# X transposed of the next Newton-Schulz iteration as a product of X and B, row loads one by one, and a new list of steps

## The chip, the cores and the metric

The kernel runs on one core of a Trainium2 chip (trn2), as one program with one launch. The metric is device time in microseconds (us). The time of the kernel before is the median of three runs. TensorE (PE in the profile; PEld is its weight loads), VectorE (DVE), ScalarE (ACT), GpSimd (POOL) and SyncE (SP, which issues all DMAs) each work through their own instruction stream in order, and wait for each other by semaphores.

## The reference: what is computed

x has 4 batches, 512 tokens and 256 columns, all float32. A layer norm is followed by two branches: causal window attention (2 heads of 128, blocks of 128 tokens), and a test-time-training layer with 16 small networks (4 batches x 4 heads, weights W0, W1, W2 of 64x64 each). Their sum goes through Wo, a layer norm and the residual; then a feed-forward part (256 to 1024 to 256, exact GELU), a layer norm and a residual. The tokens go in 4 chunks of 128. After each of the first three chunks the 48 weights are changed by a gradient that five Newton-Schulz iterations make nearly orthogonal:

```
for a, b, c in NS_COEFFS:          # five of them
    A = X @ X.T
    B = b * A + c * (A @ A)
    X = a * X + B @ X
```

The next chunk needs the new weights, so this chain (five iterations, three chunks) is serial.

## The kernel before

All data stay in SBUF. One list, ORDER (lines 136 to 183), names 687 steps such as `NA.0.1.2` (kind NA, chunk 0, iteration 1, group 2). Every engine walks through that same list and does its own part of each step; so the list sets the order on each engine, and each engine waits by semaphores for what the others make. `bank_plan` gives each step its PSUM bank, or a pair of banks, from the list; the PE part of a step waits until the bank's last reader is done (`take`, `take_pair`).

The three groups (0: W1, 1: W2, 2: W0) hold 16 matrices of 64x64 each. An iteration of a group is four steps. TX (line 670; ACT part 946) transposes X by four 128x128 matmuls against the identity, and ACT copies the result into XT. NA (681) multiplies XT by itself, DVE (1242) makes A. NB (691) squares A, DVE (1249) makes B. NX (701; ACT 950) multiplies B and X, and ACT writes the new X; in the last iteration DVE writes U (the weights plus the update) instead. NA, NB and NX are 16 logical products of 64x64, spread over the four quadrants of the array (QUADS); the profile has two records for each of them, so 32 matmul records and 32 weight loads for a step, and 4 and 4 for TX.

After the last iteration RN and RM normalize the rows of U with a square root on POOL (a power, line 1406) and small DVE operations, then WX transposes the new weights. Before the first, MU, MR, SS and SN make the Frobenius norm (POOL power) and X. Beside this chain, the list places the projections of the next chunk (XT, QK, VV, TR), attention (S, PT, PV, CT), WO, NT, and the feed-forward (F1, line 769, and F2, line 783) of this chunk, as filling for PE. The steps FW, DH, GB, OUT, EL, ELB and DW are the small networks' forward and backward parts. F2N, the last step of a row block, subtracts and scales on DVE (1370), adds the residual on POOL (1511), and SP stores the block.

SP issues the loads: x of chunk 1 (`rows_in(1)`) after the weights of the small networks, then p1T, p2T, wo and x again for the residual (`rows_again`). For later chunks `rows_in` and `rows_again` are one DMA of 512 KB each; those of chunk 3 and chunk 2 follow the four stores of chunk 0. At the start, PE does eight matmuls on a tile of ones (line 803) before its first real work.

Of the kernel before, what the change touches and what calls it, by code (L numbers as in the profile page):

```python
# [26 lines left out]
ALU = mybir.AluOpType  # L27
# [3 lines left out]
P = 128  # L31
# [3 lines left out]
HD = 64  # L35
# [39 lines left out]
class Signal:  # L75
# [53 lines left out]
def steps(text):  # L129
# [22 lines left out]
    TR.1.7 TR.1.8 NX.0.4.0 NX.0.4.1 NX.0.4.2 RN.0.0 RN.0.1 RN.0.2 RM.0.0 RM.0.1 TR.1.9 KL.1.0 KL.1.1 RM.0.2 SP.1 S.1.1
    F2.0.1 F2.0.2 DH.1 WX.1.0 WX.1.1 WX.1.2 KL.1.2 KL.1.3 F2.0.3 FE.1.0 FE.1.1 EL.1.0 EL.1.1 FW.1.0 FW.1.1 ELB.1.0
    ELB.1.1 GB.1.0 GB.1.1 OE.1 QK.2.0 QK.2.1 OUT.1.0 OUT.1.1 MU.1.0 MU.1.1 MU.1.2 MR.1.0 MR.1.1 DW.1.0 DW.1.1 PT.1.0
    PT.1.1 MR.1.2 QK.2.2 S.1.2 QK.2.3 SS.1.0 SS.1.1 OY.1 SS.1.2 S.1.3 VV.2.0 PV.1.0 SN.1.0 SN.1.1 VV.2.1 PT.1.2 PV.1.1
    PT.1.3 SN.1.2 TX.1.0.0 PV.1.2 PV.1.3 CT.1.0 CT.1.1 TX.1.0.1 TX.1.0.2 NA.1.0.0 NA.1.0.1 NA.1.0.2 WO.1.0 WO.1.1
    CT.1.2 WON.1.0 CT.1.3 WON.1.1 SI.2.0 NB.1.0.0 NB.1.0.1 NB.1.0.2 L2.1.0 NQ.2.0 L2.1.1 L2N.1.0 WO.1.2 WO.1.3 TR.2.0
    NX.1.0.0 NX.1.0.1 NX.1.0.2 TX.1.1.0 NT.1.0 VV.2.2 TX.1.1.1 TX.1.1.2 WON.1.2 NA.1.1.0 NA.1.1.1 NA.1.1.2 SI.2.1
    NB.1.1.0 NB.1.1.1 WON.1.3 L2.1.2 TR.2.1 TR.2.2 TR.2.3 VV.2.3 NB.1.1.2 L2.1.3 NX.1.1.0 NX.1.1.1 L2N.1.1 NX.1.1.2
    L2N.1.2 TX.1.2.0 TX.1.2.1 TX.1.2.2 L2N.1.3 NT.1.1 NT.1.2 NT.1.3 NQ.2.1 NA.1.2.0 NA.1.2.1 NA.1.2.2 SI.2.2 SI.2.3  # L160
    F1.1.0 F1.1.1 NQ.2.2 NQ.2.3 NB.1.2.0 NB.1.2.1 NB.1.2.2 MS.2 F2N.0.0 F2N.0.1 F1.1.2 F1.1.3 F2N.0.2 NX.1.2.0 F2N.0.3
# [5 lines left out]
    GB.2.1 PT.2.0 OY.2 EL.2.0 EL.2.1 QK.3.0 ELB.2.0 ELB.2.1 MU.2.0 MU.2.1 MU.2.2 MR.2.0 QK.3.1 MR.2.1 MR.2.2 PT.2.1
    DW.2.0 DW.2.1 QK.3.2 SS.2.0 S.2.2 S.2.3 SS.2.1 SS.2.2 PV.2.0 PV.2.1 QK.3.3 CT.2.0 CT.2.1 SN.2.0 PT.2.2 TX.2.0.0
    SN.2.1 SN.2.2 WO.2.0 TX.2.0.1 TX.2.0.2 NA.2.0.0 NA.2.0.1 NA.2.0.2 NB.2.0.0 NB.2.0.1 NB.2.0.2 VV.3.0 PT.2.3
    NX.2.0.0 NX.2.0.1 NX.2.0.2 F2N.1.0 F2N.1.1 F2N.1.2 TX.2.1.0 TX.2.1.1 WON.2.0 PV.2.2 TX.2.1.2 F2N.1.3 SI.3.0  # L170
    NA.2.1.0 NA.2.1.1 NA.2.1.2 CT.2.2 PV.2.3 WO.2.1 NB.2.1.0 NB.2.1.1 NB.2.1.2 CT.2.3 WON.2.1 WO.2.2 WO.2.3 NX.2.1.0
# [5 lines left out]
    NB.2.4.2 TR.3.4 F1.2.2 NX.2.4.0 NX.2.4.1 NX.2.4.2 RN.2.0 RN.2.1 RN.2.2 MS.3 TR.3.5 F1.2.3 F1.2.4 F1.2.5 F1.2.6
    WX.3.0 WX.3.1 WX.3.2 F1.2.7 RM.2.0 RM.2.1 RM.2.2 FE.3.0 FE.3.1 FW.3.0 FW.3.1 PT.3.0 OE.3 S.3.2 S.3.3 OUT.3.0
    OUT.3.1 PT.3.1 F2.2.0 OY.3 PV.3.0 F2.2.1 PT.3.2 PT.3.3 PV.3.1 PV.3.2 CT.3.0 PV.3.3 CT.3.1 CT.3.2 WO.3.0 WO.3.1
    WO.3.2 CT.3.3 WON.3.0 WON.3.1 L2.3.0 L2.3.1 L2N.3.0 L2N.3.1 F2.2.2 F2.2.3 NT.3.0 NT.3.1 WO.3.3 WON.3.2 WON.3.3  # L180
# [1377 lines left out]
```

## Time and profile before

| | |
|---|---|
| median of 3 runs | 387.1 us (386.88 to 387.57) |
| profiled execution, its own time | 388.49 us |
| profiled execution, span from first to last instruction | 386.7 us, granted clock 0.999 |
| busy: PE, PEld, DVE, ACT, POOL | 369.2, 294.9, 271.5, 219.2, 191.7 us |
| chain that ended last: PE | 83% of the span |

The profiled execution has 1.8 us around its span. Busy time is the time covered by at least one instruction of the engine. Ends of matmuls are modelled, so a short wait can hide under the modelled end of the matmul before it.

### The profile page before, as it was taken

The numbers are of one execution on the slowest core, as the hardware profiler recorded it, in microseconds if no ns is written. First come the engines' busy times: TensorE is split into PE (matmuls) and PEld (weight loads), VectorE is DVE, ScalarE is ACT, GpSimd is POOL, SyncE is SP. The second block draws the span as 40 slices with busy tenths as digits, with TensorE's granted clock in tenths as the row PEclk, the third lists the DMA queues.
The fourth block names the chain that finished last, engine by engine and source line by source line (L and its number), as shares of the span: only waits on it lengthen the run. The fifth ranks groups of instructions, "written<-read, shape, count | busy, mean of one in ns | idle before, by whom it ended". The sixth has DMA issues, their size and how long they took to land.

```text
span 386.7 us, 15982 instructions
## 1 busy us (share of the span) xinstructions
PE 369.2 (95%) x6758; PEld 294.9 (76%) x6758; DVE 271.5 (70%) x729; ACT 219.2 (57%) x436; POOL 191.7 (50%) x267
## 2 busy tenths in 40 slices
PE   6969999999999999999997999999999999999994
PEld 4558678866689877988577788779888756998883
DVE  4587998735589689877665976997785583676223
ACT  1798386576453467476756336674458966524410
POOL 5486952414437755473463666553362331456323
PEclk9999999999999999999999999999999999999999
DMA  5770000000000000000050000000300000000101
GB/s 153 232 234 25 3 1 3 3 4 3 3 4 2 2 3 0 4 4 4 3 159 11 4 2 2 2 3 17 99 5 3 3 4 2 1 3 0 57 14 41
DMA packets 12342, 10.85 MB, mean 28 GB/s; under 512 B 4208, under 2 KB 11760, under 8 KB 12272
## 3 DMA queue, kind: packets, MB, share of 16 engines
q1 hardware_dynamic: 12272, 9.83, 8.3%
q8 instruction: 54, 0.88, 1.0%
q14 instruction: 16, 0.13, 0.1%
HBM read 7.73 MB, written 2.10 MB: 25 GB/s over the span
## 4 chain that ended last, share of the span: by engine, by line
PE 83%; DVE 8%; issue 3%; POOL 3%; ACT 2%; POOLq 0%; DVEq 0%; ACTq 0%
PE pair L788 14%; PE pair L777 14%; PE pair L708 6%; PE pair L686 6%; PE pair L696 5%; PE pair L677 5%; PE pair L558 5%; PE pair L743 3%; PE pair L586 3%; PE pair L758 3%; PE pair L567 3%; PE pair L727 3%; PE pair L734 2%; PE pair L657 2%; PE pair L624 1%
## 5 line engine op out<-in xcount | busy, mean ns | idle before, releaser
L777 PE MATMUL pair<-xn2T,p1T 128*128 128x512 f32 (+1 forms) x160 | 59.2, 513 | 0.0
L788 PE MATMUL pair<-p2T,h 128*128 128x256 f32 x256 | 57.0, 379 | 0.0
L788 PEld LDWEIGHTS pair<-p2T,h 128*128 128x128 f32 x256 | 48.1, 190 | 6.3
L1411 POOL TENSOR_SCALAR var<-mv 128x1 f32<-128x1 f32 (+1 forms) x55 | 14.1, 256 | 67.4 <-DVE mv L1367 30.5
L1029 ACT ACTIVATE h<-pair,b 128x512 f32<-128x512 f32 (+1 forms) x40 | 24.1, 602 | 35.5 <-PE pair L777 35.5
L777 PEld LDWEIGHTS pair<-xn2T,p1T 128*128 128x128 f32 x160 | 28.8, 190 | 17.6 <-issue 15.5
L1406 POOL TENSOR_TENSOR nq<-ssq,half 128x8 f32<-128x8 f32 (+1 forms) x16 | 23.8, 1498 | 37.2 <-DVE ssq L1128 37.1
L1052 DVE SCALAR_TENSOR_TENSOR A<-pair,eye 128x512 f32<-128x512 f32 x45 | 28.5, 680 | 11.1 <-PE pair L686 11.1
L1406 POOL TENSOR_TENSOR rstd<-var,neg_half 128x1 f32<-128x1 f32 (+1 forms) x55 | 32.9, 598 | 4.6
L820 ACT ACT_TABLE_LOAD x26 | 33.4, 1283 | 2.1 <-PEq L1548 1.7
L1052 DVE SCALAR_TENSOR_TENSOR B<-pair,eye 128x512 f32<-128x512 f32 x45 | 28.4, 681 | 6.5 <-PE pair L696 6.3
L558 PE MATMUL pair<-wqkv,xnT 128*128 128x512 f32 x64 | 29.7, 600 | 0.6 <-ACT xnT L813 0.6
L708 PEld LDWEIGHTS pair<-X,B 64*64 64x64 f32 x1440 | 23.6, 134 | 7.9 <-issue 4.5
L696 PEld LDWEIGHTS pair<-A 64*64 64x64 f32 x1440 | 23.4, 134 | 6.4 <-issue 5.1
L708 PE MATMUL pair<-X,B 64*64 64x64 f32 x1440 | 25.8, 221 | 2.0 <-issue 2.0
L954 ACT ACTIVATE X<-pair 128x512 f32<-128x512 f32 x36 | 19.5, 597 | 14.3 <-PE pair L708 14.1
L686 PEld LDWEIGHTS pair<-XT 64*64 64x64 f32 x1440 | 22.8, 135 | 4.6 <-issue 4.6
L696 PE MATMUL pair<-A 64*64 64x64 f32 x1440 | 25.7, 221 | 0.2 <-DVE A L1052 0.2
L813 ACT ACTIVATE XT<-pair 128x512 f32<-128x512 f32 x45 | 24.4, 597 | 2.6 <-PE pair L677 2.5
L686 PE MATMUL pair<-XT 64*64 64x64 f32 x1440 | 25.1, 220 | 0.6 <-issue 0.6
L677 PE MATMUL pair<-ident,X 128*128 128x128 f32 x180 | 24.0, 276 | 0.0
L1406 POOL TENSOR_TENSOR fro<-ss,half 128x8 f32<-128x8 f32 x9 | 15.9, 1781 | 13.4 <-DVE ss L1223 13.4
(163 smaller groups left out, 785.7 us busy)
## 6 DMA issues: line engine op xcount, KB each, us to landing
x<-in_L_attn_x_dram SPq DMA_DIRECT2D x4, 512.0 KB, 4.3
out_dram<-rows_a SPq DMA_DIRECT2D x16, 128.0 KB, 1.7
x_in<-in_L_attn_x_dram SPq DMA_DIRECT2D x3, 512.0 KB, 4.7
p1T<-in_L_ffn_proj_dram SPq DMA_DIRECT2D x1, 1024.0 KB, 6.0
p2T<-in_L_ffn_proj_dram SPq DMA_DIRECT2D x1, 1024.0 KB, 8.3
wqkv<-in_L_attn_Wqkv_dram SPq DMA_DIRECT2D x1, 768.0 KB, 4.5
x_in<-in_L_attn_x_dram SPq DMA_DIRECT2D x4, 128.0 KB, 4.3
wo<-in_L_attn_Wo_dram SPq DMA_DIRECT2D x1, 256.0 KB, 8.6
```

The lines of the kernel that those rows point to most:

```text
L558: mm_ = pe.matmul(ps, xnT[:, k, b * P:(b + 1) * P], wqkv[:, k, 0:512], start=(k == 0), stop=(k == KC - 1))
L677: mm_ = pe.transpose(ps[:, b * P:(b + 1) * P], X[:, g, 2 * b:2 * b + 2, :], ident[:, :])
L686: mm_ = pe.matmul(BANK[bank[0] + row][64 * col:64 * col + 64, n * HD:(n + 1) * HD], xt, xt, start=True, stop=True)
L696: mm_ = pe.matmul(BANK[bank[0] + row][64 * col:64 * col + 64, n * HD:(n + 1) * HD], a, a, start=True, stop=True)
L708: mm_ = pe.matmul(BANK[bank[0] + row][64 * col:64 * col + 64, n * HD:(n + 1) * HD], B[64 * row:64 * row + 64, g, 4 * (row ^ (slot & 1)) + ...
L777: mm_ = pe.matmul(ps[:, at], p1T[:, k, n * P:(n + 1) * P], xn2T[:, k, at], start=(k == 0), stop=(k == KC - 1))
L788: mm_ = pe.matmul(ps[:, 0:DIM], h[:, n, b * P:(b + 1) * P], p2T[:, n, :], start=(n == 0), stop=(n == HC - 1))
L813: return act.activation(dst, src, ACT.Copy)
L820: act.preload_act_table_set(name)
L1029: act.activation(h[:, n, at], BANK[bank[0]][:, at], ACT.Gelu, bias=b1[:, n:n + 1]).then_inc(S["h"].sem, 1)
L1052: return dve.scalar_tensor_tensor(out=out_, in0=in0, scalar=scalar, in1=in1, op0=op0, op1=op1)
L1406: return pool.tensor_tensor(out_, in0, in1, op)
```

## The change

TX is kept for the first iteration only. For the others a new step XX makes XT of the next iteration directly from X and B, with the operands of NX exchanged (B is symmetric, so the product of X and B is the transpose of B X); it writes a pair of banks, and ACT scales it as it scales X. XX(it) and NX(it) both wait for B(it) and, from it = 1 on, for X of the iteration before. NA of the next iteration needs XX alone. SP issues each 512 KB of rows as four DMAs of 128 KB, each one after the landing of the one before (without that wait for x of chunk 1). Some small operations are dropped or moved: the scaled maximum of the scores comes straight out of the masking reduction, the sums of an epsilon in NR and SN go from DVE to POOL, RM has one operation fewer, in the last chunk F2N is done on DVE alone with its subtraction ahead of the wait for the scale, the constants come in another order, and PE does seven matmuls on ones instead of eight. ORDER is a new list of 689 steps.

```diff
-    XT.0.0 LN1.0.0 LNX.0.0 LN1.0.1 LN1.0.2 QK.0.0 LN1.0.3 LNX.0.1 XT.0.1 SI.0.0 LNX.0.2 LNX.0.3 VV.0.0 QK.0.1 XT.0.2
...
-    NX.0.1.0 NX.0.1.1 L2.0.2 L2.0.3 NX.0.1.2 NT.0.0 NT.0.1 NT.0.2 TX.0.2.0 TX.0.2.1 L2N.0.1 L2N.0.2 L2N.0.3 TX.0.2.2
-    NT.0.3 NA.0.2.0 NA.0.2.1 NA.0.2.2 F1.0.0 F1.0.1 NB.0.2.0 NB.0.2.1 NB.0.2.2 F1.0.2 NQ.1.0 NQ.1.1 F1.0.3 LN1.2
...
+    CO.0 XT.0.0 LN1.0.0 LNX.0.0 QK.0.0 LN1.0.1 LN1.0.2 LN1.0.3 XT.0.1 LNX.0.1 LNX.0.2 LNX.0.3 SI.0.0 VV.0.0 VV.0.1
+    NQ.0.0 XT.0.2 XT.0.3 QK.0.1 SI.0.1 WI.0 LN1.1 NR.0.0 VV.0.2 VV.0.3 NQ.0.1 QK.0.2 LNX.1 MS.0 SI.0.2 QK.0.3 SM.0
+    NQ.0.2 SI.0.3 NQ.0.3 XT.1 SP.0 TR.0.0 TR.0.1 TR.0.2 NR.0.1 VV.1.0 NR.0.2 NR.0.3 TR.0.3 KL.0.0 WX.0.0 WX.0.1 WX.0.2
...
+    F1.0.3 LN1.2 NX.0.1.1 NB.0.2.1 NX.0.1.2 NB.0.2.2 NX.0.2.0 NB.0.3.0 F1.0.4 XX.0.2.1 NR.1.3 XX.0.2.2 XX.0.3.0 TR.1.4
+    LNX.2 F1.0.5 KL.1.0 NA.0.3.1 NA.0.3.2 KL.1.1 KL.1.2 NA.0.4.0 XT.2 F1.0.6 NX.0.2.1 NX.0.2.2 NB.0.3.1 NB.0.3.2
...
+    F1.3.7.0 F1.3.0.1 F1.3.1.1 F2N.2.1 F1.3.2.1 F1.3.3.1 F1.3.4.1 F1.3.5.1 F1.3.6.1 F1.3.7.1 F2N.2.2 F2N.2.3 F2.3.0
+    F2.3.1 F2.3.2 F2N.3.0 F2N.3.1 F2.3.3 F2N.3.2 F2N.3.3

 def rows_again(c):
-    sp.dma_start(x1[:, c % 2, :, :], rows(c)).then_inc(S["x_again"].sem, 16)
+    for b in range(BATCH):
+        if b:
+            sp.wait_ge(*S["x_again"](c, 16 * b))
+        sp.dma_start(x1[:, c % 2, b, :], x[b, bass.ts(c, CHUNK), :]).then_inc(S["x_again"].sem, 16)

 # PE, NX: one more wait
+    if it > 0:
+        pe.wait_ge(*S["X"](c, 3 * (it - 1) + g + 1))

+def XX(bank, c, it, g):
+    take_pair(bank[0], "XT", c, 3 * (it + 1) + g + 1)
+    if it > 0:
+        pe.wait_ge(*S["X"](c, 3 * (it - 1) + g + 1))
+    pe.wait_ge(*S["B"](c, 3 * it + g + 1))
+    for n in range(4):
+        for row, col in QUADS:
+            half, k = n & 1, 2 * (n >> 1) + col
+            slot, at = ns_slot(it, g, half, k), (2 * (n >> 1) + half) * HD
+            mm_ = pe.matmul(BANK[bank[0] + row][64 * col:64 * col + 64, at:at + HD],
+                            X[64 * row:64 * row + 64, g, slot, :],
+                            B[64 * row:64 * row + 64, g, 4 * (row ^ (slot & 1)) + (slot >> 1), :], start=True, stop=True)
+    mm_.then_inc(S["xt_ps"].sem, 1)

 # ACT
+def XX(bank, c, it, g):
+    act.wait_ge(*S["xt_ps"](c, 3 * (it + 1) + g + 1))
+    act.activation(halves(XT[:, g, :, :]), both(bank[0]), ACT.Copy, scale=NS_REST[it]).then_inc(S["XT"].sem, 1)

-for n in range(8):      # PE, matmuls on ones
+for n in range(7):

 # DVE, RM: three small operations become two, with row_inv = 1 / row_norm made once (step WR)
-    dve.tensor_scalar(u_e[:, g, :], u_n[:, g, :], 1e-5, None, ALU.add).then_inc(S["u_eps"].sem, 1)
+    stt(u_e[:, g, :]..., u_n[:, g, :]..., 1e-5, row_inv[:, g, :]..., ALU.add, ALU.mult).then_inc(S["u_eps"].sem, 1)
...
-    dve.tensor_scalar(nmax[:, b, :], smax[:, b, :], -SCALE, None, ALU.mult).then_inc(S["neg_max"].sem, 1)

 # DVE, F2N of the last chunk
+    dve.tensor_scalar(f2_n[:, b, :], f2[:, b, :], mv4[:, b, 0:1], None, ALU.subtract).then_inc(S["f2_n"].sem, 1)
+    wait_apart(dve, S["f2_n"](c, b + 1))
+    dve.wait_ge(*S["f2_rstd"](c, b + 1))
+    stt(outb[:, b, :], f2_n[:, b, :], rstd4[:, b:b + 1], x1[:, c % 2, b, :], ALU.mult, ALU.add).then_inc(S["outb"].sem, 1)
```

## Rows read from the trace of the kernel before

**Rows 1.** The page: busy us (share) and count by engine.

```profile
PE 369.2 (95%) x6758; PEld 294.9 (76%) x6758; DVE 271.5 (70%) x729; ACT 219.2 (57%) x436; POOL 191.7 (50%) x267
```

**Rows 2.** Waits of PE: line, releaser: us in total, times, longest.

```profile
PE pair L542 <- DVE rows_b L1081: 2.3, 1, 2.3
PE pair L708 <- issue: 2.0, 1, 2.0
PE pair L586 <- POOL silu L1406: 1.3, 1, 1.3
...
PE pair L686 <- issue: 0.6, 1, 0.6
```

**Rows 3.** Waits of the weight loads (PEld), same columns.

```profile
PEld pair L708 <- DVE B L1052: 2.8, 5, 0.8
```

**Rows 4.** The chain in order of time: start us, us, what.

```profile
59.63 1.67 PE pair L686 x96
...
66.31 1.09 PE pair L708 x64
...
79.67 1.31 PE pair L677 x12
...
94.16 1.72 PE pair L777 x4
...
98.04 1.56 PE pair L686 x96
99.60 3.63 PE pair L777 x8
...
104.78 1.86 PE pair L708 x96
```

**Rows 5.** Timeline, 0 to 34 us: start us, us, engine, instruction [idle before].

```profile
3.06 3.75 PE L803 MATMUL pair<-ones 128*128 128x128 f32 x16 [3.06 <-DVE ones L1389]
...
5.35 0.41 DVE L1074 TENSOR_SCALAR rows_b<-x_in,mv,rstd 128x256 f32<-128x256 f32 x1 [1.12 <-POOL rstd L1406]
...
12.25 0.59 SPq L457 DMA_DIRECT2D x_in<-in_L_attn_x_dram  x1
...
19.70 1.36 DVE L1064 BATCH_NORM_STATS2 st<-x_in 128x6 f32<-128x256 f32 x4
```

**Rows 6.** The page, DMA issues: count, KB each, us to landing.

```profile
x_in<-in_L_attn_x_dram SPq DMA_DIRECT2D x3, 512.0 KB, 4.7
```

**Rows 7.** Timeline, 374 us to the end, same columns.

```profile
382.15 0.18 DVE L1367 BATCH_NORM_AGGREGATE mv<-st 128x2 f32<-128x6 f32 x1
...
383.40 0.41 DVE L1372 TENSOR_SCALAR rows_a<-rows_a,mv,rstd 128x256 f32<-128x256 f32 x1 [1.07 <-POOL rstd L1406]
383.89 0.72 POOL L1406 TENSOR_TENSOR rows_a<-rows_a,x 128x256 f32<-128x256 f32 x1 [0.53 <-DVE rows_a L1372]
```

**Rows 8.** Groups of instructions: names xcount | busy us, mean ns | idle.

```profile
L1134 DVE TENSOR_SCALAR nqe<-nq 128x8 f32<-128x8 f32 x12 | 5.6, 470 | 0.7 <-POOL nq L1406 0.7
...
L1289 DVE TENSOR_SCALAR nmax<-smax 128x2 f32<-128x2 f32 x16 | 3.2, 198 | 0.6
```

**Rows 9.** Timeline, 196 to 209 us: row loads, and the wait of PE.

```profile
198.01 0.46 SPq L452 DMA_DIRECT2D x<-in_L_attn_x_dram  x1
...
198.52 0.54 SPq L457 DMA_DIRECT2D x_in<-in_L_attn_x_dram  x1
...
205.72 1.63 PE L708 MATMUL pair<-X,B 64*64 64x64 f32 x96 [2.03 <-issue]
```

**Rows 10.** The page, DMA queues over the span: packets, MB, share.

```profile
q8 instruction: 54, 0.88, 1.0%
```

**Rows 11.** The DMA view of 197.2 to 203.2 us, same columns.

```profile
q1 hardware_dynamic: 1324, 1.29, 70.5%
```

**Rows 12.** The DMA view of 203.2 to 204.3 us, same columns.

```profile
q8 instruction: 1, 0.02, 5.6%
```

**Rows 13.** Busy by engine, 264 to 304 us: length, PE, PEld, DVE, ACT, POOL, clock.

```profile
264.00:304.00 40.00, 40.00 (x1244) 34.61 (x1240) 28.90 (x74) 24.08 (x47) 16.90 (x29) 1.00 0.10 30
```

More of the change, by code:

```diff
@@ L152 @@
[L152 to L161, printed above, removed]
@@ L167 @@
[L167 to L171, printed above, removed]
@@ L177 @@
[L177 to L180, printed above, removed]
-    L2.3.2 L2.3.3 L2N.3.2 L2N.3.3 F1.3.0.0 F2N.2.0 F2N.2.1 F2N.2.2 F2N.2.3 F1.3.1.0 F1.3.2.0 F1.3.3.0 F1.3.4.0
@@ new lines @@
+    LNX.2 F1.0.5 KL.1.0 NA.0.3.1 NA.0.3.2 KL.1.1 KL.1.2 NA.0.4.0 XT.2 F1.0.6 NX.0.2.1 NX.0.2.2 NB.0.3.1 NB.0.3.2
+    F1.0.7 NX.0.3.0 NB.0.4.0 XX.0.3.1 XX.0.3.2 TR.1.5 TR.1.6 TR.1.7 TR.1.8 MP.1 WR.0 SP.1 KL.1.3 TR.1.9 NA.0.4.1
+    NA.0.4.2 F2.0.0 NX.0.3.1 NX.0.3.2 NX.0.4.0 NB.0.4.1 NB.0.4.2 F2.0.1 NX.0.4.1 RN.0.0 RN.0.1 NX.0.4.2 RN.0.2 RM.0.0
+    RM.0.1 RM.0.2 F2.0.2 F2.0.3 F2N.0.0 WX.1.0 WX.1.1 WX.1.2 DH.1 FW.1.0 FW.1.1 FE.1.0 FE.1.1 EL.1.0 EL.1.1 GB.1.0
+    GB.1.1 ELB.1.0 ELB.1.1 OUT.1.0 OUT.1.1 PT.1.0 OE.1 QK.2.0 QK.2.1 QK.2.2 DW.1.0 DW.1.1 MU.1.0 MU.1.1 MU.1.2 MR.1.0
@@ L188 @@
           "F1": 1, "F2": 1, "SS": 1, "TX": 1, "WX": 1}
-PAIRED = ("NA", "NB", "NX", "GB", "FW", "DH", "OUT")
+PAIRED = ("NA", "NB", "NX", "XX", "GB", "FW", "DH", "OUT")
 def last_reader(step, n):
@@ L1048, in _ @@
         def _(dve):
+            dve.memset(ones[:, :], 1.0).then_inc(warm, 1)
             for name in RAISED_AHEAD["vector"]:
@@ L1052, in stt, with CO @@
                 return dve.scalar_tensor_tensor(out=out_, in0=in0, scalar=scalar, in1=in1, op0=op0, op1=op1)
+            def CO(c):
+                dve.memset(small_bias[:, 0:12], BASE_LR_INV)
+                dve.memset(ones_avg[:, :], 0.5 / CHUNK)
+                for r in range(2):
+                    for k in range(2):
+                        last = dve.memset(ones_blk[64 * r:64 * r + 64, 64 * k:64 * k + 64], float(r == k))
+                last.then_inc(prepared, 1)
             def LN1(c, b=None):
@@ L1387, in run @@
                         parts[kind](c, *arg)
-            dve.memset(ones[:, :], 1.0).then_inc(warm, 1)
-            dve.memset(neg_half[:, :], -0.5)
-            dve.memset(half[:, :], 0.5)
-            dve.memset(small_bias[:, 0:12], BASE_LR_INV)
-            dve.memset(ones_avg[:, :], 0.5 / CHUNK)
-            for r in range(2):
-                for k in range(2):
-                    last = dve.memset(ones_blk[64 * r:64 * r + 64, 64 * k:64 * k + 64], float(r == k))
-            last.then_inc(prepared, 1)
             run(ORDER)
```

139 lines of the change are left out of this document (78 added, 61 removed).

## The prediction

> **What bounds the kernel now.** I read the page's busy row first, then the waits of PE, then the chain in order of time, and the timeline where the chain leaves PE. The row shows PE covered for 369.2 of 386.7 us and DVE for 271.5 [rows 1]. So the time is PE's own work plus the places where PE waits. The waits of PE [rows 2] are few: at the start for the normalized rows of chunk 1 (2.3 us) and for POOL's scaled q and k (1.3), and in the middle 2.0 and 0.6 us of "issue", waits that no semaphore explains. The weight loads [rows 3] show what the modelled ends of matmuls hide: 2.8 us in 5 places behind DVE's B. The start (first real matmul at 6.6 us) and the tail behind the last matmul (5.6 us) are serial and have their own chains.
>
> **PE's own work.** The chain gives step prices [rows 4]: three quadrant steps in a row take 1.56 us, two take 1.09, so one more costs 0.47. Three transpose steps TX take 1.31, so 0.44 each. XX replaces TX 36 times (iterations 0 to 3, 3 groups, 3 chunks): 36 x 0.03 = +1.1 us. XX has the matmuls of NX, 16 products on quadrants, and I price it as NX; exchanging the two operands leaves all shapes at 64x64. From below: TX's own price, +0. From above: a step of a triple with the slow spacing, 1.86 / 3 = 0.62 [rows 4], +6.5. I take 0.47, the undisturbed row.
>
> A run of quadrant steps between steps on the whole array costs something at its borders. F1 after a quadrant triple: two steps in 3.63 us, where one alone takes 1.72, so 0.19 for the borders, and the triple takes 1.56 where 3 x 0.47 is 1.41, so 0.15 more: 0.34 us a run [rows 4]. Counting both lists, the quadrant steps (NA, NB, NX, XX, FW, DH, OUT) stand in 51 runs in the old one and in 57 in the new one: +2.0 us. That XX does away with the whole-array TX inside an iteration does not pay here, because the new list spreads the groups more finely. Together PE's work grows by 3.1 us. The Trainium skill says the same of the borders (TensorEngine Tiling (Array Packing), Key Properties: a change of tiling mode drains the engine), and speaks against this change, as it would against any list with more runs; it names no price, and the 0.34 is the trace's.
>
> PE also has one more semaphore wait ahead of NX and up to two ahead of XX (63 in all for the X of the iteration before). That X was written by ACT one iteration earlier, several us of PE work ago, so nothing is waited for. The instruction itself is taken in ahead of the matmuls: nothing, at most 0.05 us each, the difference of two such borders, so 3 us at most.
>
> **Start.** The first transpose starts at 6.61, though its rows are written at 5.35 + 0.41 = 5.76: it stands behind the eight matmuls on ones, 3.75 us long [rows 5]. One less is 3.75 / 8 = 0.43 to 0.47 us earlier, just what the rows allow: -0.4 us, if the clock is granted as before. After it PE runs without a wait to about 18.7 (its work there is the same as now, where it first waits at 18.3). Now XT.1 comes next instead of TR.0.0. Its rows: x of chunk 1 is issued from 12.25 on and lands 4.7 us later [rows 5, 6], near 17; statistics on DVE 1.36 + 0.4 [rows 5], two small POOL operations 1.3, normalization on DVE as long as the statistics, the copies of VV lying between: about 21.9. So PE waits 3.2 us in one place and 1 us for ACT's copy behind it, and TR.0.0 to TR.0.2 are queued behind the waiting XT.1 though they are ready. Against that, the waits before XT.1 (2.3) and TR.0.4 (1.3) go [rows 2], with a shorter one before TR.0.0, and three VV steps fill the time for POOL's chain, which gets 4 additions of 0.26 us longer. Followed further by the same durations (EL and ELB now ahead of OE on DVE, so DW is 1.5 us earlier against the work; OE ahead of MU, so the momentum is later), NA.0.0.0 comes out at 59.5, as now at 59.63 [rows 4]. So: 0, between -1.5 and +1.5.
>
> **Tail.** Before: aggregate 382.15 + 0.18, POOL's scale, DVE 383.40 + 0.41, POOL 383.89 + 0.72 = 384.61, then the store [rows 7]. Now F2N.3.2 follows F2.3.3 on DVE, two operations of 0.41, then F2N.3.3's subtraction and product, again 2 x 0.41: from 382.4 with three gaps, 384.2. -0.4 us, between -0.8 (F2N.3.2 fits in earlier) and 0.
>
> **Small operations.** DVE loses 16 maxima of 0.2 us, 16 additions of 0.47 [rows 8], and some 18 of 0.16; about 12 us of its busy time. PE does not wait for most of them; the long ones (0.47 is a mean over 0.15 and about 1 us) hold A and B back in a dense place. I count this in the next part. POOL gets 25 additions of 0.26 and is half idle: 0. RM's saved operation lies in a chain for which the new list leaves 7.8 us or more of other PE work against about 5.8: 0.
>
> **Waits in the iterations.** This is where the change can win. (a) Row loads: two 512 KB DMAs are issued at 198.01 and 198.52, and PE, with no semaphore open, stands still for 2.03 us before 205.72 [rows 9]. From 197.2 to 203.2 only the queue of the data has packets [rows 11]; one packet of the queue "instruction" follows at 203.2 to 204.3 [rows 12]. The kernel has 54 of them, 0.88 MB [rows 10], for 2 x 6758 PE instructions [rows 1], so one per 250. I read it as PE's code waiting behind the rows. With at most 128 KB under way this cannot last: -2.0 us; from above 0, if the code is late for another reason. (b) Consumers close behind producers: by the step prices, 51 places in the old list have under 1.3 us of PE work between the end of NA, NB, NX or TX and the step that needs it (a DVE or ACT operation of 0.6 to 0.68 and two hand-overs take about 1.0), 17 in the new one. What that costs shows in the triple at 104.78, 1.86 instead of 1.56, and in rows 3: 2.8 us of B waits, and some for A. Part of these lies under matmuls still draining; between 0.3 (what the matmul rows show) and 4 I take 2.4 now and 0.8 after: -1.6. Fewer close places come from the shorter chain, since NA needs XX alone and NX can come late.
>
> Sum: 3.1 - 0.4 + 0 - 0.4 - 2.0 - 1.6 = -1.3 us. The profiled span of 386.7 becomes 385.4, its own time of 388.5 becomes 387.2; the median of the runs, 387.1, becomes 385.8. About 0.2% (0.8 us) is what a measurement tells from no change.
>
> **Rivals.** First, PE's code becomes the bound, and the kernel is slower. XX has 64 matmuls and weight loads where TX has 8: +56 x 36 = 2016 instructions, 8 blocks more, all in the iterations. In the 40 us from 264 to 304 PE has 1244 matmul and 1240 load records [rows 13], a block in 4.0 us, and no such wait. The wait of 0.6 us inside an NA step [rows 2], with no row load near, says that a denser stretch (there about 3.1 us for a block) is already too fast. With 56 more for each XX the mean there falls to about 3.3 us for a block. If a block needs 3.7 (0.6 more than 3.1), the mean shortfall is 0.4, but only where the list is dense: of some 45 blocks in the iterations I count 12, 4.8 us, which come on top of -1.3, less 0.6 for close places that the waits then cover: 390.0. It decides from a block time under about 3.5 us on. For it: the 0.6 us, and runs of six to nine quadrant steps in the new list. Against it: that wait is one in 54 blocks. The Trainium skill (Runtime: NRT & Kernel Launch, Instruction fetch mechanics) calls the cost of passing from one 16 KiB block to the next mostly hidden; by that rule this rival is worth nothing and the 2.0 us are due to something else, but the trace's two waits disagree.
>
> Second, the gains cancel: the 2.0 us are not the row loads' doing, or the wait returns elsewhere. Now the four loads of rows take about 4 x 2.2 us one after the other, twice, next to the densest steps of chunk 1. Then 3.1 - 0.8 - 1.6 + 0.6 = +1.3 at most, and with half of it 387.2. For it: a single wait is the evidence.
>
> Third, the start goes better than followed: three VV steps earlier leave PE ahead of DVE, and 1.5 to 2 us of the start's waits go: 384.0. Against it: DVE is nearly full from 40 to 60 us, and its order sets the first X.
>
> That XX does not shorten the chain at all can be left out: NA's wait is on XT alone, and one PE step and one ACT copy are gone from each iteration.
>
> **Chances.** The forecast 0.44, with its own range 384.5 to 387.0; code as the bound 0.28 (387.8 to 392); cancelled 0.20 (386.4 to 388.2); a better start 0.08. Faster by over 0.2%, below 386.3: 0.35 + 0.08 + 0.03 = 0.46; within 0.2%: 0.09 + 0.13 + 0.02 = 0.24; slower: 0.30. Range for 8 in 10: 383.2 to 390.5; it leaves out the worse part of the first rival and the sum of all lower bounds.
>
> **What would show it.** PE's busy count must rise by about 2000 matmul and load records and the instruction queue by 8 packets. Right: XX triples at 1.56 us; no wait of PE over 1 us while rows are loaded; NA.0.0.0 near 59.5; the end 5.2 us behind the last matmul. The first rival shows as "issue" waits of PE in front of or inside NA, NB, NX and XX, of 3 us or more in total, each with an instruction packet shortly before its end. A dearer XX (0.5 or more), or a start over 1.5 us later, would also make the prediction wrong.

## The result, and the profile after

The changed kernel takes 396.65 us (median of three runs, 395.9 to 399.36) against 387.1 us before (386.88 to 387.57): ratio 1.0235, interval 1.0191 to 1.0279. It is slower by 9.5 us and lies outside the range of the prediction (383.2 to 390.5). Its profiled execution has a span of 394.5 us, 7.8 us more than before, and 2.15 us around it. Here and below, ratios and intervals are taken over the fast runs alone (in e1, e3 and e4 one run of four was slow), so a ratio is not the quotient of the two medians.

The page after, in its busy row and the row of the instruction queue, to be read beside [rows 1] and [rows 10]:

```profile
PE 375.5 (95%) x7764; PEld 298.1 (76%) x7764; DVE 261.1 (66%) x682; ACT 216.7 (55%) x433; POOL 194.4 (49%) x290
...
q8 instruction: 62, 1.02, 1.1%
```

PE has 1006 matmuls and as many weight loads more, and eight instruction packets more, as forecast. DVE lost 10 us. The waits of PE, as in [rows 2]:

```profile
PE pair L544 <- DVE rows_b L1111: 3.3, 1, 3.3
...
PE pair L695 <- issue: 1.4, 1, 1.4
PE pair L695 <- ACT XT L974: 1.0, 1, 1.0
PE pair L709 <- issue: 0.8, 1, 0.8
PE pair L676 <- DVE X L1263: 0.6, 2, 0.3
PE pair L560 <- ACT xnT L829: 0.6, 1, 0.6
PE pair L781 <- DVE A L1073: 0.5, 1, 0.5
```

L695 is NB and L709 NX in the changed kernel. The 2.0 us before NX are gone; in their place stand 1.4 and 0.8 us of "issue" and 1.0 us behind ACT's copy of XT, all in chunk 2. The iterations of chunk 2, from NA.2.0.0 to NX.2.4.2, in the windows of the kernel before (columns as in [rows 13]):

```profile
263.00:312.90 49.90, 49.90 (x1557) 41.80 (x1560) 35.62 (x93) 33.15 (x62) 18.31 (x32) 1.00 0.08 25
```

The same stretch of the kernel after:

```profile
263.30:319.50 56.20, 52.22 (x1887) 43.05 (x1887) 35.44 (x89) 31.06 (x61) 17.30 (x33) 1.00 0.03 9
```

PE was covered throughout before and has 4 us of holes after, with nothing busier than it. The largest hole, in the timeline of the changed kernel:

```profile
273.24 1.04 PE L695 MATMUL pair<-A 64*64 64x64 f32 x43
...
275.68 0.98 PE L695 MATMUL pair<-A 64*64 64x64 f32 x51 [1.40 <-issue]
```

It lies inside the step NB.2.1.0, which waits for semaphores only ahead of its first matmul, so no semaphore can be the cause: the step's first part is done, and its next record starts 1.6 us later.

**A place in the instruction stream.** If all of PE's records are numbered from 0 in order of start (matmuls, weight loads, and the semaphore instructions, which the page doesn't count: 13945 before, 15964 after), the waits of over 0.7 us in the iterations that no semaphore explains have one thing in common:

| kernel | wait ends at record | modulo 256 | us between starts |
|---|---|---|---|
| before | 1985 | 193 | 0.79 |
| before | 7873 (the 2.0 us of [rows 9]) | 193 | 2.10 |
| after | 11969 | 193 | 1.62 |
| after | 14017 | 193 | 1.00 |

The instruction queue has 62 packets of 16 KB for the 15964 records after (257 for each) and 54 for the 13945 before (258 for each). I read it so: every 256 records PE crosses into a block of code whose packet must be there. I call the place a crossing. The numbering starts at the first record that the trace shows, and instructions ahead of it would shift it; so the period of 256 says something, and the 193 by itself does not. The packet of the wait at 275.68 had run from 272.92 to 274.22 (DMA view of 272.9 to 274.3 us of the kernel after):

```profile
q8 instruction: 1, 0.02, 5.8%
```

From 274.2 to 275.6 no queue had a packet at all, and PE went on 1.46 us after its packet had ended. The two waits of chunk 2 have the same sequence: the packet starts 1.1 to 1.4 us after the crossing ahead of it, takes 0.9 to 1.3 us, and 1.2 to 1.5 us after its end PE goes on. In the iterations of both kernels the crossings are 3.45 us apart at the least, and nearly all 3.6 or more: **a block costs about 3.7 us at least**, on the mean of a dense stretch. That is an estimate and no hard floor: single blocks are shorter in the experiments (down to 1.9 us in e3 and e4, 2.9 in e1, 3.2 in e12), and the 86 blocks of all traces that end in a wait of over 0.3 us take 4.0 in the median, since a packet can also start late. Eight quadrant steps of 64 instructions take 3.7 us and hold two blocks.

The Trainium skill (Runtime: NRT & Kernel Launch, Instruction fetch mechanics) calls the cost of crossing a block mostly hidden. The traces agree where 256 instructions last longer than that (all crossings of the kernel before but two, whose packets started 2.3 and 3.8 us after the crossing ahead); in runs of quadrant steps they do not.

**Where the 7.8 us are.** I took the time between the first matmuls of neighbouring steps, less the step prices of the prediction and 0.34 us for each run of quadrant steps. From NA.0.0.0 on:

| us | before | after |
|---|---|---|
| places over 0.12 us with a crossing in them | 3.7 | 4.4 |
| places over 0.12 us without one | 2.1 | 7.3 |

Besides these there are +1.1 us of work for XX, six runs more (+2.0 by the price of the prediction, which nothing measures by itself), -0.2 at NA.0.0.0 (59.63 to 59.45) and -0.4 in the tail. That adds up to 8.4 us, 0.6 more than measured. The crossings hide a change of kind: the 1.9 us beside the row loads went, and 2.8 us came in chunk 2. The places without a crossing are 1.24 us in one (NB.2.3.0, whose banks wait for ACT's copy of XT), and some twenty of 0.12 to 0.6 us, half of them in chunk 2.

### The profile page after: what moved, and what is told of

Same layout as the page of the kernel before. It is cut to its first block, busy times and chain, and to the rows that moved or that the text cites. A ratio compares the mean times of both kernels' runs of the same rounds, so it can differ in the third digit from the quotient of the medians.

```text
span 394.5 us, 17995 instructions
## 1 busy us (share of the span) xinstructions
PE 375.5 (95%) x7764; PEld 298.1 (76%) x7764; DVE 261.1 (66%) x682; ACT 216.7 (55%) x433; POOL 194.4 (49%) x290
## 4 chain that ended last, share of the span: by engine, by line
PE 74%; DVE 9%; issue 5%; POOL 4%; ACT 3%; SPq 3%; DMA 1%; POOLq 0%; DVEq 0%; ACTq 0%
PE pair L793 13%; PE pair L804 12%; PE pair L695 5%; PE pair L709 5%; PE pair L685 5%; PE pair L724 4%; PE pair L588 4%; PE pair L560 4%; PE pair L774 3%; PE pair L759 3%; PE pair L743 3%; PE pair L569 2%; PE pair L750 2%; POOL rstd L1430 2%; PE pair L659 1%
## 5 line engine op out<-in xcount | busy, mean ns | idle before, releaser
L1435 POOL TENSOR_SCALAR var<-mv 128x1 f32<-128x1 f32 (+1 forms) x55 | 12.2, 222 | 79.2 <-DVE mv L1393 43.8
L1073 DVE SCALAR_TENSOR_TENSOR B<-pair,eye 128x512 f32<-128x512 f32 x45 | 29.9, 685 | 18.9 <-PE pair L695 18.6
L709 PEld LDWEIGHTS pair<-X,B 64*64 64x64 f32 x1440 | 24.8, 135 | 8.6 <-issue 7.0
L695 PE MATMUL pair<-A 64*64 64x64 f32 x1440 | 28.2, 220 | 2.9 <-issue 1.4
L709 PE MATMUL pair<-X,B 64*64 64x64 f32 x1440 | 28.8, 221 | 0.8 <-issue 0.8
L970 ACT ACTIVATE X<-pair 128x512 f32<-128x512 f32 x36 | 20.9, 596 | 15.3 <-PE pair L709 15.3
L974 ACT ACTIVATE XT<-pair 128x512 f32<-128x512 f32 x36 | 20.3, 596 | 14.8 <-PE pair L724 14.7
L695 PEld LDWEIGHTS pair<-A 64*64 64x64 f32 x1440 | 24.7, 135 | 4.7 <-issue 2.8
L685 PE MATMUL pair<-XT 64*64 64x64 f32 x1440 | 27.2, 221 | 0.5 <-DVE wo_n L1346 0.2
L1430 POOL TENSOR_TENSOR kl<-silu,lr 128x256 f32<-128x256 f32 x24 | 14.3, 618 | 25.6 <-issue 25.6
L1389 DVE TENSOR_TENSOR rows_a<-pair,b 128x256 f32<-128x256 f32 x16 | 6.6, 415 | 27.1 <-PE pair L804 27.1
```

The lines of the kernel that those rows point to most:

```text
L685: mm_ = pe.matmul(BANK[bank[0] + row][64 * col:64 * col + 64, n * HD:(n + 1) * HD], xt, xt, start=True, stop=True)
L695: mm_ = pe.matmul(BANK[bank[0] + row][64 * col:64 * col + 64, n * HD:(n + 1) * HD], a, a, start=True, stop=True)
L709: mm_ = pe.matmul(BANK[bank[0] + row][64 * col:64 * col + 64, n * HD:(n + 1) * HD], B[64 * row:64 * row + 64, g, 4 * (row ^ (slot & 1)) + ...
L970: act.activation(halves(X[:, g, :, :]), both(bank[0]), ACT.Copy, scale=NS_REST[it]).then_inc(S["X"].sem, 1)
L974: act.activation(halves(XT[:, g, :, :]), both(bank[0]), ACT.Copy, scale=NS_REST[it]).then_inc(S["XT"].sem, 1)
L1073: return dve.scalar_tensor_tensor(out=out_, in0=in0, scalar=scalar, in1=in1, op0=op0, op1=op1)
```

## The experiments

Each ran beside the kernel before on the same chip; the ratio is to it. "From NA.0.0.0 to the end" is the time from that step's first matmul to the end of PE's work in the profiled execution: 321.5 us before, 329.9 after. It leaves the start out.

**e1, the crossings shifted.** Against the kernel before:

```diff
-for n in range(8):   pe.matmul(BANK[7][...128...], ones, ones)
+for n in range(6):   pe.matmul(BANK[7][...128...], ones, ones)
+for n in range(26):  pe.matmul(BANK[7][0:64, 0:64], ones[0:64, 0:64], ones[0:64, 0:64])
```

> The kernel before, with its eight matmuls on ones at the start replaced by six of them and 26 small ones of 64x64. That puts 96 more PE instructions ahead of the first real one, in about the same 3.6 us; list, waits and work are unchanged. Theory S (supply of PE's instructions): in both traces the waits of PE over 0.7 us that no semaphore explains end at the same place of its instruction stream, counted in all PE records: 193 modulo 256 (records 1985 and 7873 before; 11969 and 14017 after; one at 13484 is at 172). So every 256 instructions PE crosses into a block that must have been fetched, and between two crossings at least about 3.7 us must pass. Shifting the crossings by 96 puts several of them into dense runs of quadrant steps. Worked out from the step prices: +11 us, 398, with single waits of 1.3 to 1.9 us inside steps near NX.0.3.2, NX.1.3.2, NB.2.0.1 and NB.2.3.2, each again at 193 modulo 256. Rival L (what costs is the list: borders between quadrant and whole-array steps, consumers close behind producers): list and steps are unchanged, so 387.1 within 0.5 us.

Measured: 408.4 us, ratio 1.045 (1.036 to 1.054). The profiled execution is the fastest of the four (402.8 us; the others took 408.3 to 409.6, and no trace shows where their last 5.6 us are). In it NA.0.0.0 to the end takes 333.4 us, 11.9 more than before (forecast 11); the first matmul came 2.5 us later besides. Twelve waits over 0.3 us end at 193 modulo 256, 13.5 us together. The waits of PE:

```profile
PE pair L696 <- issue: 3.7, 3, 1.7
PE pair L708 <- issue: 3.1, 4, 1.8
PE pair L686 <- issue: 2.4, 3, 1.0
```

All four steps named have a wait in them (0.6, 2.0, 1.1 and 1.3 us between starts). Rival L is out: with an unchanged list the time grew by more than the change itself had cost.

**e2, the control: a whole block more.** 4 matmuls on ones and 68 small ones.

> The kernel before with 256 more small PE instructions at the start (four matmuls on ones and 68 of 64x64 instead of eight on ones), one whole block. The control for the shift of 96: more instructions, but every crossing at the same step as before. Theory S: 387.1 to 387.8 (the small matmuls may end 0.3 us later than the eight). If added instructions cost by themselves, it is slower than the shift of 96.

Measured: 404.3 us, ratio 1.039 (1.033 to 1.045), but not for the crossings: from NA.0.0.0 to the end it takes 322.3 us, 0.8 more than before, and the only wait over 0.3 us at a crossing is the one of the row loads (1.83 us). The time was lost at the start, in the timeline:

```profile
5.03 14.77 PE L805 MATMUL pair<-ones 64*64 64x64 f32 x136
19.73 0.28 PEld L535 LDWEIGHTS pair<-ident,rows_b 128*128 128x128 f32 x2
```

My padding was 13 us dearer than planned, and NA.0.0.0 comes another 2.7 us later against it. As to its question the control holds: 256 instructions more don't cost in the body, 96 do.

**e3, the changed kernel shifted by 64.** 5 matmuls on ones and 18 small ones instead of 7.

> The changed kernel with 64 more PE instructions at the start (five matmuls on ones and 18 of 64x64 instead of seven on ones), the rest unchanged. Theory S: the crossings come 64 instructions earlier in the list, and now the dense runs of all three chunks hold one; worked out from the step prices +20 us or a little less, 412 to 418. Rival L: 396.6 within 0.5 us.

Measured: 413.4 us, ratio 1.062 (1.056 to 1.067), as forecast. From NA.0.0.0 on 344.9 us, 15.0 more than the changed kernel; 16 waits at 193 modulo 256, 19.0 us. Seven are in NB:

```profile
PE pair L695 <- issue: 7.9, 7, 1.5
PE pair L724 <- issue: 3.7, 4, 1.4
```

So the list as it stands suits one position of its crossings. Four instructions fewer, as the change has with seven matmuls on ones in place of eight, should not matter: by the same working a shift of up to some 50 in that direction is nearly free, and 16 the other way costs 6 us. Neither was run.

**e4, XX alone.** The kernel before, TX.c.it+1.g taken out and XX.c.it.g put ahead of NX.c.it.g:

```diff
-... NX.0.1.0 NX.0.1.1 L2.0.2 ... TX.0.2.0 TX.0.2.1 ...
+... XX.0.1.0 NX.0.1.0 XX.0.1.1 NX.0.1.1 L2.0.2 ...
```

> The kernel before with one thing of the change: TX of the iterations 1 to 4 is gone, and XX stands directly ahead of NX of the same group. List otherwise, row loads, small operations as before. 51 runs of quadrant steps as before, PE's work by the step prices +1.1 us. Theory S: eight more blocks, all in the dense runs, 20 or more crossings under 3.7 us: +18 to +27 us, 405 to 415. Rival L (the new list is what costs, XX itself only 36 times 0.03): 387 to 388.5. Rival C (the shorter chain helps where the list is as before): 385 to 387.

Measured: 413.5 us, ratio 1.062 (1.055 to 1.069). From NA.0.0.0 on 346.1 us, 24.6 more than before, and 24 waits at crossings sum to 25.0 us. Two of them, in the timeline (L692 is NB, L704 NX, L719 XX here):

```profile
211.95 0.62 PE L692 MATMUL pair<-A 64*64 64x64 f32 x25
214.29 1.29 PE L692 MATMUL pair<-A 64*64 64x64 f32 x71 [1.73 <-issue]
...
216.24 0.51 PE L704 MATMUL pair<-X,B 64*64 64x64 f32 x18
218.65 0.59 PE L704 MATMUL pair<-X,B 64*64 64x64 f32 x12 [1.90 <-issue]
```

Between two waits lie 256 records and about two microseconds of work. XX by itself is what is dear, by its number of instructions and not by its matmuls. With the new list (and the rest of the change) 24.6 becomes 8.4; but e3, the same list shifted by 64, stands at 23.4. So the runs do not tell how much the new list gains by putting filling between the dense steps and how much by the position of its crossings.

**e5, the row loads one by one, alone.** The `rows_in` and `rows_again` of the change's diff in the kernel before.

> The kernel before with only the row loads of the change: four of 128 KB one after another in place of each 512 KB. Theory S (PE needs a fetched block every 256 instructions): the crossing at 203.62 waited 2.10 us because its packet started only at 203.25, 3.8 us after the crossing before it, behind the two loads; with 128 KB under way at most it starts within 1 to 2 us, as the others do. So the wait goes and nothing takes its place: -2.0 us, ratio 0.995. If the loads are not the cause, or it returns at a later crossing: ratio 1.000 within 0.001.

Measured: 398.1 us, ratio 1.023 (1.018 to 1.027): slower by 9 us (by 7.2 in the trace from NA.0.0.0 on). Theory S was right on the crossing (no wait at 193 is left) and blind to what follows. The timeline of SyncE and VectorE:

```profile
200.41 7.18 SPq L455 DMA_DIRECT2D x<-in_L_attn_x_dram  x4
207.63 7.75 SPq L463 DMA_DIRECT2D x_in<-in_L_attn_x_dram  x4
...
217.08 1.41 DVE L1070 BATCH_NORM_STATS2 st<-x_in 128x6 f32<-128x256 f32 x4 [9.71 <-DMA x_in<-in_L_attn_x_dram]
...
219.66 1.13 PE L692 MATMUL pair<-XT 64*64 64x64 f32 x32 [8.10 <-issue]
```

Eight loads, in two sets of four in which each waits for the landing of the one before it, take 15 us. The rows of chunk 3 are there at 217 and not near 204; DVE waits 9.7 us for them, with A and lr queued behind, and NA waits 8.1 us (named "issue", at record 50 modulo 256, so no crossing).

**e6 and e7, the small parts.** e6 is the changed kernel with the old list, TX and 512 KB loads; e7 the same with the loads one by one.

> The changed kernel with the old list and without XX (TX in all iterations, no wait for X ahead of NX) and with the old 512 KB loads: what is left of the change is the small operations, the last chunk's F2N on DVE, the order of the constants and seven matmuls on ones instead of eight. Five PE instructions more than before in all (by the program), so the crossings lie as before. Expected -0.4 at the start, -0.4 in the tail, some 0 to 0.7 us of B and A waits from 12 us less on DVE: -0.8 to -1.5 us, ratio 0.996 to 0.998.

> All of the change but XX and the new list: small operations, tail, start and the row loads one by one, on the old list. If the parts add up: -2.0 and -0.8 to -1.5, so -2.8 to -3.5 us, ratio 0.991 to 0.993, and faster than both kernels. If the row loads' wait comes back elsewhere: as the kernel with the small operations alone.

Measured: e6 389.2 us, ratio 1.000 (0.997 to 1.003); e7 397.8 us, ratio 1.022 (1.017 to 1.027). Both expectations were wrong. The start (6.18 instead of 6.61) and the tail showed their 0.4 us in e6's trace, but its median didn't; e7 has e5's wait, 9.0 us between starts. One thing that eats the gain in e6's trace is the clock: 0.9 us behind the end of its wait of 1.9 us at the row loads, PE's granted clock falls to half (1.2 GHz of 2.4), where the kernel before has 1.00 behind its own wait of 2.1 us. The windows of e6:

```profile
205.40:208.80 3.40, 3.40 (x67) 3.28 (x58) 1.14 (x7) 2.40 (x5) 1.26 (x2) 0.50 0.02 5
```

The iterations of chunk 1 take 58.9 us there and 57.4 before. A stretch at 0.50 stands behind the waits at this place in e1, e2 and e4 too, and a longer one around the 8 and 9 us waits of e5 and e7. So a wait of PE can cost more than its own length.

**e8, the changed kernel with 512 KB loads.**

> The changed kernel with the row loads undone (512 KB each again). In the changed kernel the loads run from 170.4 to 185.7 us, beside crossings 4 us apart that have 0.3 to 0.4 us to spare. Theory S: the two large loads hold an instruction packet back by 3 us, so +1.5 to +3 us, 398 to 399.7, with one wait of 1.5 to 3 us at 193 modulo 256 between 170 and 185 us. If the size of the loads does not matter here: 396.6 within 0.5.

Measured: 396.9 us, ratio 1.020 (1.016 to 1.024), no different from the changed kernel. Its trace shows the wait forecast at crossing 27, but 0.88 us of it and not 1.5 to 3 (0.32 in the changed kernel). The new list has the stores, and so the loads, at 170 us and not at 198, so neither size of load comes late. That the loads one by one didn't do in the change what they do in e5 is the list's merit.

**e9 and e10, the load earlier.** Against the kernel before (e10: against e6):

```diff
 for c in range(CHUNKS - 2):
-    rows_in(c + 2)
+    if c == 0:
+        rows_in(2)
+        rows_in(3)
     stores(c)
```

> The kernel before with one line of SyncE moved: the 512 KB load of x for chunk 3 is issued ahead of the stores of chunk 0 (as soon as the rows of chunk 2 are normalized, near 110 us) and not behind them at 198.5. Only the second load for the residual stays at 198. Theory S with what the row loads one by one taught (the loads must be early, not small): the instruction packet at 203.25 starts about 2 us earlier, the 2.1 us wait at 203.6 goes, and VectorE has its rows long before it reads them: -1.8 to -2.1 us, ratio 0.995. If a load of 512 KB alone already holds the packet back: -0.5 or less, ratio 0.999 to 1.000.

> The same move with the small operations, the tail and the seven matmuls on ones of the change, on the old list with TX and loads of 512 KB. The small operations alone gave a ratio of 1.000 (0.997 to 1.003), so this should be as the move alone: -1.8 to -2.5 us, ratio 0.994 to 0.996, and the fastest of all kernels so far.

Measured: e9 386.9 us, ratio 0.997 (0.994 to 1.000), with 319.5 us from NA.0.0.0 on, 2.0 less than before: the forecast is met in the trace and in the medians (388.9 before on that chip), but the ratio says 1.2 us and its interval just reaches 1. e10 387.25 us, ratio 0.994 (0.992 to 0.997): **faster than both kernels**, by 2.2 us against before by the ratio and 1.6 by the medians; whether it beats e9 is not decided. Its twelve runs all have a granted clock of 0.997 or 0.998, where those of the kernel before beside it lie between 0.988 and 1.0; so a part of the gain may be the clock's. No wait of PE at a crossing over 0.3 us is left in its body; in e9 one is:

```profile
PE pair L688 <- issue: 0.6, 1, 0.6
```

**e11, chunk 2 back to the old list.** The changed kernel up to NA.2.0.0, then the old list with TX, and its crossings put where the step prices like them best.

> The changed kernel up to the first NA of chunk 2, and from there the old list with TX (672 PE instructions fewer), the last chunk's tail as in the change. Five matmuls on ones and 56 small ones on the four quadrants in turn at the start, so that the crossings fall where the step prices give the least stalls: 2.8 us in all, where the changed kernel has 6.8 by the same working. Theory S: 0.7 us less work and 4.0 us less stall than the changed kernel: near 392, ratio 1.010 to the kernel before. If chunk 2 is not where the change loses (rival: start and borders): 396.6 as the changed kernel.

Measured: 392.5 us, ratio 1.0075 (1.004 to 1.011): the time is as forecast. From NA.2.0.0 to NX.2.4.2 50.3 us, against 56.2 in the changed kernel and 50.0 before. So chunk 2 is where the change loses. But the reason given, 4 us fewer stalls at crossings, is not what its trace shows: the waits over 0.3 us there sum to 4.3 us in all, against 2.9 in the changed kernel and 4.4 in e13, the same program again. In chunk 2 they are 1.7 us, against 2.6 and 4.8; in chunks 0 and 1, where the shift moved them, they are more. The old list takes away XX's instructions and the new list's semaphore waits together, so e11 tells where, and not which of the two.

**e12, XT.1 behind TR.0.2.**

> The changed kernel with XT.1 moved behind TR.0.2, so that the ready transposes TR.0.0 to TR.0.2 run while the rows of chunk 1 are made. In the changed kernel PE waits 3.3 us for them, and then shows a granted clock of 0.72 from 22 to 28 us and transposes of twice the duration. If the start's loss reaches the end: -1 to -2 us, 394.6 to 395.6, no stretch under full clock in the start. If VectorE sets the first iteration anyway (NA.0.0.0 at 59.5 in both kernels): 396.6 within 0.5, and NA.0.0.0 within 0.5 us of 59.5.

Measured: 401.7 us, ratio 1.032 (1.029 to 1.036), 5 us slower than the changed kernel: outside both expectations. ACT now works on TR's tables and copies when XT.1 is ready, and PE waits longer for its copy:

```profile
PE pair L568 <- ACT xnT L828: 4.5, 1, 4.5
```

From NA.0.0.0 to the end nothing changed (330.0 us); NA.0.0.0 came at 63.3, against 59.4 in the changed kernel and 58.9 in e13. So it was not VectorE alone that set it, and the change's order of the start is the better one.

**e13 to e15, supply or semaphores in chunk 2.** e13 is the changed kernel again; e14 moves one filling step, e15 brings in another.

```diff
-... NX.2.2.0 NB.2.2.2 NB.2.3.0 F1.2.0 F2N.1.1 ...
+... NX.2.2.0 F1.2.0 NB.2.2.2 NB.2.3.0 F2N.1.1 ...           e14
+... NX.2.2.0 F1.2.0 NB.2.2.2 NB.2.3.0 F1.2.1 F2N.1.1 ...    e15
```

> The changed kernel itself, unchanged, as the base on the same chip for the two that follow: 396 to 398 us.

> The changed kernel with one filling step moved: F1.2.0 stands ahead of NB.2.2.2 instead of behind NB.2.3.0, two steps earlier. Open question: between NA.2.0.0 and NX.2.4.2 the changed kernel has 3854 PE instructions, 15.1 blocks, at 3.7 us a block 55.7 us, and takes 56.2. But waits at crossings (2.6 us) are only part of what it lost there; 1.24 us is a wait of NB.2.3.0 for ACT's copy of XT, which holds its banks, and about 1 us are smaller semaphore waits. Theory S (the supply sets the time there, other waits only lie within it): the 1.24 us wait goes, since 1.9 us of F1 now stand ahead of it, and a crossing a little later waits 1.2 to 1.9 us in its place; the stretch stays at 56.0 to 56.3 and the time at that of the changed kernel within 0.3 us. Rival B (the new list's semaphore waits are the cost by themselves): the stretch takes 55.0 and the kernel is 1.2 us faster.

> As the kernel before this one, and one F1 step more among the iterations of chunk 2: F1.2.0 ahead of NB.2.2.2, F1.2.1, F1.2.2 and F1.2.3 where F1.2.0, F1.2.1 and F1.2.2 stood; F1.2.3 is taken from behind NX.2.4.2, where five such steps cover the row norms. It brings 8 PE instructions and 1.9 us of work into the dense stretch. Theory S: the stretch grows by 0.3 to 0.8 us only, since the work fills what were waits for the supply, and the part behind it is 1.9 us shorter: -1.0 to -1.6 us against the changed kernel, unless WX.3 now waits for the norms. Rival B: the stretch grows by 1.9 less 1.2 us for the wait that goes, and the kernel is 1.2 us faster as well; the two kernels together tell them apart by the one before.

Measured: 397.5, 396.7 and 397.2 us; ratios 1.020 (1.017 to 1.024), 1.019 (1.014 to 1.023), 1.019 (1.015 to 1.023). The stretch from NA.2.0.0 to NX.2.4.2 took 58.6, 56.4 and 58.8 us. The wait for ACT's copy went in both:

```profile
PE pair L723 <- ACT h L1048: 1.1, 1, 1.1
PE pair L694 <- issue: 0.9, 1, 0.9
PE pair L708 <- issue: 0.9, 1, 0.9
```

These are the rows of e14, where another semaphore wait of the same size took its place, 3 us later. In e15 1.9 us more work and 1.24 us less of that wait lengthened the stretch by 0.2 against e13, while its waits at crossings stayed (4.8 and 4.9 us); the part behind it won 0.3 and not 1.9, since a crossing waited there (1.2 us of PE, 1.9 between starts). No gain of 1.2 us shows, which speaks against rival B, but the intervals (0.4% each way) and the base's own spread (56.2 and 58.6 us for one program) don't settle 1 us. Of the 2.4 us of that spread 2.2 lie in waits at crossings; without these waits the stretch takes 53.5 to 53.9 us in the changed kernel, e13, e14 and e15 alike.

## Why the prediction was wrong, by its own steps

**PE's own work, +1.1 and +2.0: held as far as it shows.** XX triples take 1.56 us, as priced, and the step prices sum to 1.1 us more. The 2.0 for the runs was not measured by itself. The row of the chain after:

```profile
85.55 1.56 PE pair L724 x96
```

The extra waits for X cost nothing that shows.

**Start and tail: held in their ends, not in the way.** First real matmul 6.15, NA.0.0.0 at 59.45 (forecast 59.5), the end 5.2 us behind the last matmul (5.2). PE's wait for XT.1 was 3.3 us (3.2). The sum has a slip: it takes -0.4 for the earlier first matmul, but the start, followed to NA.0.0.0, brought only 0.1 of it (59.63 to 59.5; measured 0.2). What I left out is the clock: right behind that wait the granted clock fell, and the next three TR steps took nearly twice their time.

**(a) Row loads, -2.0: held in the change, for another reason.** The wait at the crossing is gone, and e9 shows that the loads had held the packet back. But the step "with at most 128 KB under way this cannot last" looked at the crossing alone. It did not ask when the last of eight serial loads lands; on the old list that costs 9 us (e5). In the change the loads are issued at 170 us and not at 198, behind earlier stores, and that covers it.

**(b) Close places, -1.6: failed, in sign and size.** I counted places with less than 1.3 us of work between producer and consumer, and their fall from 51 to 17 did lower the waits for B (weight loads: 2.8 us before in NX, 0.8 after in XX). But the count looked at NA, NB, NX and TX alone. In the new list waits of other kinds appear: a bank still held by ACT's copy of XT (1.24 us), rows for NT (0.5 and 0.6), sums of squares for SS (0.5), X for TX (0.6 in two). All waits without a crossing rose by 5.2 us where they should have fallen by 1.6.

**The supply of PE's instructions: not in the sum.** The sum has no term for it; it stood only in the first rival, given 0.28 and 390.0: the mechanism that happened, taken too small. The rival's block time of 3.7 us was right, and so was the sign. Wrong was how it was applied: as a mean shortfall of 0.4 us in 12 blocks guessed. A crossing is a point in the list: what counts is the work between one record 193 modulo 256 and the next, block by block. Done so from the step prices, with the semaphore instructions counted in, it gives 0.35 us of stalls for the old list and 6.8 for the new. It leaves out all semaphore waits, which lie in the same blocks; so for the new list it is more than the traces show at crossings (2.9 us in waits over 0.3 us, 4.4 in e13). A simpler sum would have done as well: from NA.2.0.0 to NX.2.4.2 the new list has 3854 PE instructions, 15.1 blocks, 55.7 us at 3.7; it took 56.2. The old one has 3194, 46.2 us at 3.7, under the 50.0 it took. In chunks 0 and 1 the same sum gives 57.5 against 65.7 and 65.4 us, so only where the crossings fall matters there. The argument against the rival, that the trace had one such wait in 54 blocks, showed only that the old list had its crossings in good places; e1 shows what it is worth without them.

The forecast's -1.3 and the measured +7.8 us of span differ by 9.1, by these sums: 6.8 from (b), 2.7 from the crossings (+0.7 where -2.0 was forecast) and 0.2 from the start, less the 0.6 us that the sums are too high. The step that failed is thus "Waits in the iterations", forecast at -3.6 us and measured at +5.9. Most of it is in chunk 2: the stretch from NA.2.0.0 to NX.2.4.2 is 6.2 us longer, of which less than 1 us is work by the step prices.

(b) and the crossings are not independent, because waits inside a block count towards its 3.7 us: with all semaphore waits gone, chunk 2's stretch would still take 55.7. By that bound about 5.7 of the 6.2 us are the supply's, or 4.2 with 3.6 us for a block. Taken the other way, the waits seen at its crossings are 2.6 us (4.8 in e13), and without them 3.6 us of the 6.2 are left. So the share of the supply in chunk 2 is argued, between 2.6 and 5.7 us, with e1 to e4 for the block time. e11 won 4.2 us in the medians by going back to the old list with TX in chunk 2, which takes away both causes; e14 and e15 fit the bound without proving it. What stays open besides is the rest outside chunk 2, some 3 us against the forecast, in small waits of the new list: no run takes them apart.

## What to carry to other kernels

Count instructions as well as microseconds: where an engine's instructions are short, the stream's supply is a bound of its own (here 256 PE instructions per 3.7 us, 14.5 ns each, while a quadrant step issues one in 7.3), and an edit that trades 8 instructions for 64 must be priced by it. A tuned list holds its crossings in good places, and an edit that shifts the count of instructions ahead of them can cost 10 us with no other change (e1, e3); look at unexplained waits by their record number modulo 256 first. A load that competes with the supply should be issued early, not cut into pieces that wait for each other.

## What the runs showed of the hardware that I had not expected

- The supply's period: 65 waits of PE over 0.6 us end at record 193 modulo 256, in fourteen of the seventeen traces. The other waits of that size in the iterations stand where a step waits for a semaphore, or (e5, e7) between matmuls at half clock.
- Small 64x64 matmuls on one and the same quadrant, all into the same place of a PSUM bank, take 14.77 us for 136 records (e2), 109 ns each, and 3.30 us for 52 (e1), 63 ns each; in e11, on the four quadrants in turn and into changing places, 3.27 us for 112, 29 ns each; 15 ns in a quadrant step of 64 instructions. No run separates the quadrant from the place written, nor from the clock: four QK matmuls behind the padding take 3.75 us in e2 and 1.95 in e1. The timeline of e11:

```profile
5.47 3.27 PE L824 MATMUL pair<-ones 64*64 64x64 f32 x112
```

- After its idle time of 3.3 us in the start, PE ran at half its clock: the windows of the changed kernel from 22.3 to 27.1 us show a granted clock of 0.64, so much of that time at 1.2 GHz instead of 2.4, and three TR steps together take 2.77 us of PE where they took 1.47 before.

```profile
22.30:27.10 4.80, 4.80 (x24) 4.49 (x25) 1.81 (x7) 4.51 (x9) 4.43 (x7) 0.64 0.24 74
...
23.22 2.77 PE L588 MATMUL pair<-ident,raw 128*128 128x128 f32 x12
```

- The start is not the same in every execution of one program. The first QK step, in the timelines of the changed kernel and of e13, which is the same program:

```profile
7.10 1.95 PE L560 MATMUL pair<-wqkv,xnT 128*128 128x512 f32 x4 [0.56 <-ACT xnT L829]
...
7.38 3.75 PE L560 MATMUL pair<-wqkv,xnT 128*128 128x512 f32 x4 [0.56 <-ACT xnT L829]
```

  Nearly twice the time for the same four matmuls looks like half clock, though the clock column shows 1.00 there in both. It bears on small differences: e10's trace has the slow form and NA.0.0.0 at 61.3 us, e6's the quick one and 58.9.
